# Cross attention with a recurrent scan: a shorter warm-up over states kept by column, an earlier check, and a projection that runs five groups ahead

## The chip, the cores and the metric

One core of a Trainium2 chip runs the kernel. Its engines work beside each other: TensorE (PE, matmuls; PEld is its weight load), VectorE (DVE), ScalarE (ACT), GpSimd (POOL), and SyncE (SP), which issues DMAs. The metric is the device time in microseconds; lower is better.

## The reference

x (4096 tokens of 512) attends with 8 heads to a context of 3202 tokens; a second layer norm follows, a projection to 64 numbers per token, and a recurrence over all tokens:

```python
x = residual + _mha(layernorm(x), layernorm(ctx), W_qkv, b_qkv, W_o, b_o)
residual = x
U = (layernorm(x) @ W_in.T + b_in) @ Bmat            # [T, 64]
def step(s, u_t):
    s = silu(s @ A.T) + u_t
    return (s, s)
_, states = scan(step, zeros, U)
x = residual + states @ Cmat
return x + (ctxb.mean(axis=1) @ W_prog.T + b_prog)
```

## The kernel before, in words

Attention comes first, 32 units of 512 queries and a pair of heads. Its outputs are scaled by the reciprocal of the sum of weights, split into a high and a low part (ost) and stored to o_scratch. The last unit's output is still on its way when the next stage begins: fold_den, invert and spread_rden turn its sum, scale_o (GpSimd) scales, high_o (ScalarE) and low_o (GpSimd) split, store_o (SP) stores. Groups 14 and 15 of the next stage can be loaded only after that store.

**Projection stage**, 16 groups (d) of 256 tokens, each in two halves. SP loads og(d), the attention output, into one of 3 slots, and x into xb. GpSimd adds the output bias to xb (add_bias). TensorE projects (24 matmuls, two PSUM banks; each half waits until VectorE has emptied the half before). VectorE adds xb into x1 and runs the norm's statistics and 13 tiny operations (an inverse root), which give the scale ya and the bias nmr. ScalarE applies them (norm2, into the one xn), TensorE transposes (turn2), ScalarE copies to nt (take_n2), and for every second group TensorE multiplies by w_u (finish) and ScalarE writes u twice (take_u): to u_low, the lower half of su, and to u_high. In TensorE's order project(d+3) stands before turn2(d). Some small work is hung on given groups: the sum over ctxb (VectorE, L1024), its matmuls, and c1, c2.

**Scan.** 4096 tokens are 256 chunks (NCH) of 16 (LCH). Step k handles token k of all chunks at once: a matmul of [u; v] (the 128 partitions of su) by A twice stacked, then a silu into v of the next column. Halves of 128 chunks alternate between two banks. The first sweep starts each chunk from zero; column 15 hands its result to the next chunk's column 0; the second sweep repeats all columns from there, and VectorE adds u to v for the states. A check compares the last column's v of both sweeps with 2^-38 of the squared norm of the states, by a matmul with ones, and writes a flag. All three engines read it; if it fails, the 4095 steps run one by one. Last, the states are split (s1, s2), multiplied with c1, c2, added to x1 and stored.

What orders all this is each engine's own queue, written out by hand, with semaphores.

## Time and profile before

| | |
|---|---|
| median of 3 runs | 2356.67 us (2354.91 to 2357.35) |
| profiled execution | 2354.21 us, its span 2351.9 us |
| attention, up to the projection | 2118.6 us |
| projection stage with its tail | 2118.6 to 2279.4 |
| scan | 2279.4 to 2316.0 |
| check and flag | 2316.0 to 2323.0 |
| final sums and stores | 2323.0 to 2351.9 |
| mean granted clock of TensorE | 0.98 |

The time of an execution is its span plus what lies around it. Busy time alone says little here: each stage has its own limit. The stages' borders are read from the timeline.

### The profile page before, as it was taken

The page shows a single profiled execution, that of the slowest core. Times are in us where ns is not written, and L with a number is a line of the kernel's source. Part 1 is how long each engine was busy: PE and PEld are TensorE (multiplying, and loading weights), DVE is VectorE, ACT ScalarE, POOL GpSimd, SP SyncE. Part 2 cuts the span into 40 slices and gives each one's busy share as a digit, 9 for nine tenths or more (in the row PEclk, how much of TensorE's full clock was granted, in tenths as well). Part 3 has the DMA queues.
Part 4 walks back from the last instruction along what each step waited for, and adds up shares of the span by engine and source line. Part 5 has one row for each costly group of instructions (what it writes and reads, how often), then busy time and mean ns, then how long its engine had stood idle before and what let it go on. Part 6 is the DMA issues. An engine that isn't in the chain of part 4 may idle for free.

```text
span 2351.9 us, 35969 instructions
## 1 busy us (share of the span) xinstructions
PE 2277.1 (97%) x14148; PEld 1321.2 (56%) x14148; DVE 1732.7 (74%) x2167; ACT 1121.4 (48%) x1429; POOL 1583.7 (67%) x1039
## 2 busy tenths in 40 slices
PE   8999989999999999999999999999999999998877
PEld 8998854555555545555555555555555555446653
DVE  5865546788888777888888887888887888646645
ACT  3654424454444444544454444544444445542354
POOL 1200026888888888888888889888888888884201
PEclk8999999999999999999999999999999999999987
DMA  6650225777677777776777777776777767877513
GB/s 241 217 177 10 81 74 120 155 155 156 155 154 160 172 164 171 174 159 153 164 158 178 165 174 170 155 155 154 156 157 159 155 154 162 188 174 220 171 45 143
DMA packets 158678, 365.01 MB, mean 155 GB/s; under 512 B 22511, under 2 KB 62063, under 8 KB 157870
## 3 DMA queue, kind: packets, MB, share of 16 engines
q0 software_dynamic: 59904, 218.13, 45.4%
q1 hardware_dynamic: 98606, 144.58, 19.0%
q8 instruction: 112, 1.84, 0.3%
q14 instruction: 56, 0.46, 0.1%
HBM read 95.41 MB, written 49.02 MB: 61 GB/s over the span
## 4 chain that ended last, share of the span: by engine, by line
PE 83%; POOL 4%; DMA 4%; issue 4%; DVE 3%; ACT 2%; SPq 0%; ACTq 0%; DVEq 0%; POOLq 0%
PE ps L1269 28%; PE ps L1142 10%; PE ps L1244 7%; PE ps L1246 7%; PE ps L1248 7%; PE ps L1106 4%; PE ps L1236 4%; DMA acca<-pt 3%; POOL accp L526 3%; PE ps L1124 3%; PE ps L1114 3%; PE ps L1333 2%; PE ps L1390 1%; PE ps L1087 1%; DVE mx_part L892 1%
## 5 line engine op out<-in xcount | busy, mean ns | idle before, releaser
L708 ACT ACTIVATE pt<-ps 128x1024 f32<-128x1024 f32 x800 | 779.1, 1021 | 909.3 <-PE ps L1248 886.1
L892 DVE TENSOR_REDUCE mx_part<-ps 128x2 f32<-128x1024 f32 x768 | 938.5, 1222 | 347.6 <-PE ps L1142 347.6
L526 POOL TENSOR_TENSOR accp<-accp,pt 128x1024 f32<-128x1024 f32 x416 | 1037.1, 2493 | 233.4 <-ACT pt L708 230.9
L1269 PE MATMUL ps<-pt,v 128*64 128x512 f32 x3328 | 805.9, 605 | 0.0
L965 DVE TENSOR_TENSOR ps<-ps,shb 128x1024 f32<-128x1024 f32 x403 | 493.2, 1224 | 51.8 <-PE ps L1248 51.8
L1269 PEld LDWEIGHTS ps<-pt,v 128*64 128x64 f32 x3328 | 202.2, 136 | 344.2 <-issue 336.4
L1142 PE MATMUL ps<-kk,qh 64*128 64x512 f32 x1536 | 350.0, 451 | 9.9 <-DVE mx_part L892 9.9
L1142 PEld LDWEIGHTS ps<-kk,qh 64*128 64x128 f32 x1536 | 143.5, 183 | 367.2 <-DVE mx_part L892 266.6
L1244 PE MATMUL ps<-qh,kk 64*128 64x512 f32 x1664 | 329.4, 391 | 4.9 <-ACT pt L708 4.9
L1248 PE MATMUL ps<-ql,kk 64*128 64x512 f32 x1664 | 329.7, 390 | 0.0
L1246 PE MATMUL ps<-qh,kk 64*128 64x512 f32 x1664 | 329.5, 391 | 0.0
L536 POOL DMA_DIRECT2D acca<-pt x192 | 182.5, 950 | 3.7 <-ACT pt L708 1.8
L1244 PEld LDWEIGHTS ps<-qh,kk 64*128 64x128 f32 x1664 | 157.9, 185 | 40.0 <-ACT pt L708 6.6
L1246 PEld LDWEIGHTS ps<-qh,kk 64*128 64x128 f32 x1664 | 158.2, 185 | 34.7
L1248 PEld LDWEIGHTS ps<-ql,kk 64*128 64x128 f32 x1664 | 158.2, 185 | 34.0
L1236 PE MATMUL ps<-sh,ones_row 64*128 64x512 f32 x858 | 173.9, 402 | 1.1 <-ACT pt L708 1.1
L515 POOL MEMSET sh<- 128x512 f32 x2 | 1.0, 530 | 187.2 <-PE ps L1124 187.2
L546 POOL DMA_DIRECT2D accb<-pt x128 | 126.3, 987 | 0.0
L1333 PE MATMUL ps<-wo_hl,og 128*128 128x512 f32 x384 | 98.8, 415 | 16.6 <-DVE x_first L1008 12.0
L1333 PEld LDWEIGHTS ps<-wo_hl,og 128*128 128x128 f32 x384 | 74.9, 199 | 38.5 <-issue 22.9
L571 POOL TENSOR_TENSOR xb<-xb,bo 128x512 f32<-128x512 f32 x32 | 40.7, 1324 | 81.0 <-DMA xb<-x 81.0
L1236 PEld LDWEIGHTS ps<-sh,ones_row 64*128 64x128 f32 x858 | 82.6, 187 | 15.2 <-ACT pt L708 12.5
(150 smaller groups left out, 1941.6 us busy)
## 6 DMA issues: line engine op xcount, KB each, us to landing
acca<-pt POOLq DMA_DIRECT2D x224, 512.0 KB, 4.9
accb<-pt POOLq DMA_DIRECT2D x160, 512.0 KB, 4.8
q_scratch<-kk SPq DMA_DIRECT2D x32, 512.0 KB, 4.4
acca<-accp POOLq DMA_DIRECT2D x32, 512.0 KB, 4.6
o_scratch<-ost SPq DMA_DIRECT2D x32, 512.0 KB, 3.1
og<-o_scratch SPq DMA_DIRECT2D x32, 512.0 KB, 5.8
shb<-m_scratch SPq DMA_DIRECT2D x31, 512.0 KB, 4.2
xs<-x SPq DMA_DIRECT2D x16, 512.0 KB, 6.5
```

Source lines behind the costliest of these rows:

```text
L526: nc.gpsimd.tensor_tensor(acc[:, :], acc[:, :], pt[n % PT_SLOTS][:, :], ALU.add).then_inc(added_p, 1)
L536: nc.gpsimd.dma_start(acc[:, :], pt[n % PT_SLOTS][:, :], accum_op=ALU.add).then_inc(added_a[u % 2], 16)
L708: nc.scalar.activation(pt[n % PT_SLOTS][:, :], src, ACT.Exp, scale=SCALE).then_inc(exped, 1)
L892: nc.vector.tensor_reduce(mx_part[:, m % QT, :, m // QT], src, AX_X, ALU.max).then_inc(max_taken, 1)
L965: nc.vector.tensor_tensor(ps[:, b:b + 2, :], ps[:, b:b + 2, :], shb[u % 2][:, :, :], ALU.add)\
L1142: ins = mm(ps[:, bank, :], q[r, (m % QT) * P:(m % QT + 1) * P], kk[r, p, 0, a:a + QB], start=True, stop=True)
L1236: ins = mm(ps[:, 2 * (t % 2) + h, :], ones_row[r, :], sh[u % 2][r, :], start=first, stop=not first)
L1244: mm(ps[:, b + h, :], kk[r, p, 0, key], qh[u % 3][r, :], start=first, stop=False)
L1246: mm(ps[:, b + h, :], kk[r, p, 1, key], qh[u % 3][r, :], start=False, stop=False)
L1248: ins = mm(ps[:, b + h, :], kk[r, p, 0, key], ql[u % 2][r, :], start=False, stop=last)
L1269: ins = mm(ps[HD * h:HD * (h + 1), 6, :], v[:, t, f:f + HD], pt[n % PT_SLOTS][:, h * QB:(h + 1) * QB], start=(t == 0), stop=(t == NT - 1))
L1333: ins = mm(ps[:, 2 + t, :], og[:, d % OG_SLOTS, a, k, rows], wo_hl[:, b, k], start=(i == 0), stop=(i == len(PASSES) - 1))
```

## The change

The first sweep begins at column 4 (SCAN_FROM) with v = 0, so 27 steps run instead of 31. su holds column k of all chunks side by side; take_u writes u_low in that order. The silu of column 4 (of zeros, so zeros) stands in ScalarE's queue after group 12. TensorE starts when the u_low copies are there. The check's bound comes from the first sweep's last column and its sum is begun early; the first two groups of states are split before the flag is read, and the fallback, which now has its own tile su_seq, splits them again. In the projection stage project runs 5 groups ahead, scales have 6 slots, VectorE adds group 1 before it norms group 0, and the small work hangs on other groups. OG_SLOTS stays at 3. The bodies of the fallback and the new semaphores' names are left out:

```diff
@@ -31,6 +31,8 @@
 
 X_SLOTS = 8
 OG_SLOTS = 3
+AHEAD = 5
+LN_SLOTS = 6
 
 QB = 512
 QT = QB // P
@@ -84,6 +86,9 @@
 
 LCH = 16
 NCH = T // LCH
+WARM = 12
+SCAN_FROM = LCH - WARM
+SCAN_TO = 2 * LCH - 1
 TOL2 = 2.0 ** -38
 
 MOD_LO = 96
@@ -219,9 +224,9 @@
         mv = small[:, 12:16].rearrange("p (t s) -> p t s", t=GT)
         ve = small[:, 16:18]
         yi = small[:, 18:20].bitcast(I32)
-        ya = small[:, 20:24].rearrange("p (s t) -> p s t", s=2)
+        ya = at("ya", [P, LN_SLOTS, GT], RR + 11776)
         yb = small[:, 24:26]
-        nmr = small[:, 26:30].rearrange("p (s t) -> p s t", s=2)
+        nmr = at("nmr", [P, LN_SLOTS, GT], RR + 11792)
         cu = [small[0:SD, 30:31], small[SD:2 * SD, 30:31]]
         pad = small[:, 31:32]
         bqkv = small[:, 32:44].rearrange("p (w c) -> p w c", w=3)
@@ -234,7 +239,8 @@
         bvb = at("bvb", [P, FC, P], 19456)
         x1_first = at("x1_first", [P, 10 * GT, H], 19968)
         x1_last = at("x1_last", [P, 6 * GT, H], 0)
-        su = at("su", [P, T + LCH], 30208)
+        su = at("su", [P, T], 30208)
+        su_seq = at("su_seq", [P, T], 10752)
         nt = at("nt", [P, 2, FC, GW], 34320)
         xn = at("xn", [P, GT, H], 36368)
         work = at("work", [P, 1024], 37392)
@@ -262,11 +268,13 @@
         u_low, v_all = su[0:SD, 0:T], su[SD:2 * SD, 0:T]
         end1 = work[SD:2 * SD, 0:NCH]
         diff = work[SD:2 * SD, NCH:2 * NCH]
-        ends2 = work[0:SD, 512:512 + NCH]
-        excess = work[0:SD, 768:768 + NCH]
-        uv_steps = su[:, 0:T].rearrange("p (c k) -> p k c", k=LCH)
-        v_steps = v_all.rearrange("p (c k) -> p k c", k=LCH)
-        v_next = su[SD:2 * SD, LCH:T + LCH].rearrange("p (c k) -> p k c", k=LCH)
+        ends = work[0:SD, 512:512 + NCH]
+        bound = work[0:SD, 768:768 + NCH]
+        excess = xn[0:SD, 0, 0:NCH]
+        u_tokens = u_low.rearrange("p (k c) -> p c k", c=NCH)
+        uv_steps = su[:, :].rearrange("p (k c) -> p k c", c=NCH)
+        v_steps = v_all.rearrange("p (k c) -> p k c", c=NCH)
+        v_seq = su_seq[SD:2 * SD, :]
         u_steps = u_high[SD:2 * SD, :].rearrange("p (c k) -> p k c", k=LCH)
         s_steps = s_all[0:SD, :].rearrange("p (c k) -> p k c", k=LCH)
 
...
@@ -462,7 +470,7 @@
                     load_og(d)
                 sp.wait_ge(x1_ready, GT * (d - 1))
                 load_x2(d)
-                if d == 6:
+                if d == 8:
                     fold_den(UNITS - 1)
                 if d == 7:
                     sp.dma_start(cb_sb[:, :, :], ctxb).then_inc(mod_loaded, 16)
@@ -471,7 +479,7 @@
                     sp.dma_start(c_aug[0:SD, :], cmat).then_inc(mod_loaded, 16)
                     for half in (0, 1):
                         sp.dma_start(at_sb[half * SD:(half + 1) * SD, :], a_t).then_inc(mod_loaded, 16)
-                if d == 9:
+                if d == 11:
                     spread_rden(UNITS - 1)
                 if d == 13:
                     store_o(UNITS - 1)
@@ -591,9 +599,9 @@
                 send_sum(u)
             for d in range(2, X_G):
                 add_bias(d)
-                if d == 10:
+                if d == 11:
                     scale_o(UNITS - 1)
-                if d == 12:
+                if d == 13:
                     low_o(UNITS - 1)
 
 
@@ -747,7 +755,7 @@
                 wait(act, n2_turned, 2 * d)
                 for t in range(GT):
                     ins = nc.scalar.activation(xn[:, t], x1(d)[:, t], ACT.Identity,
-                                               bias=nmr[:, d % 2, t:t + 1], scale=ya[:, d % 2, t:t + 1])
+                                               bias=nmr[:, d % LN_SLOTS, t:t + 1], scale=ya[:, d % LN_SLOTS, t:t + 1])
                 ins.then_inc(normed2, 1)
 
             def take_n2(d):
@@ -759,11 +767,16 @@
 
             def take_u(i):
                 act.wait_ge(u_done, i + 1)
-                for out_ in (u_low, u_high[SD:2 * SD]):
-                    for a in (0, 1):
-                        col0 = (2 * i + a) * GW
-                        ins = nc.scalar.activation(out_[:, col0:col0 + GW], ps[SD * a:SD * (a + 1), 6, 0:GW], ACT.Identity,
-                                                   bias=cu[a])
+                for a in (0, 1):
+                    d = 2 * i + a
+                    ins = nc.scalar.activation(u_tokens[:, d * GW // LCH:(d + 1) * GW // LCH, :],
+                                               ps[SD * a:SD * (a + 1), 6, 0:GW].rearrange("p (c k) -> p c k", k=LCH),
+                                               ACT.Identity, bias=cu[a])
+                ins.then_inc(u_low_ready, 1)
+                for a in (0, 1):
+                    d = 2 * i + a
+                    ins = nc.scalar.activation(u_high[SD:2 * SD, d * GW:(d + 1) * GW], ps[SD * a:SD * (a + 1), 6, 0:GW],
+                                               ACT.Identity, bias=cu[a])
                 ins.then_inc(u_ready, 1)
 
             for d in range(X_G):
@@ -773,8 +786,11 @@
                 take_n2(d)
                 if d == 0:
                     take_den(UNITS - 1)
-                if d == 6:
+                if d == 5:
                     high_o(UNITS - 1)
+                if d == 12:
+                    act.wait_ge(v_cleared, 1)
+                    nc.scalar.activation(v_steps[:, SCAN_FROM, :], v_steps[:, 0, :], ACT.Silu).then_inc(v_started, 1)
                 if d == 13:
                     act.wait_ge(mod_ready, 1)
                     act.wait_ge(c_cleared, 1)
@@ -784,28 +800,41 @@
             take_u(X_G // 2 - 1)
 
 
-            for k in range(2 * LCH - 1):
-                if k == 2 * LCH - 2:
-                    act.wait_ge(cmp_step, 1)
+            for k in range(SCAN_FROM, SCAN_TO):
+                if k == SCAN_TO - 1:
+                    act.wait_ge(cmp_step, 2)
                 for h, c in scan_halves():
-                    act.wait_ge(z_done, 2 * k + (h + 1))
-                    out_ = v_next[:, 0, c] if k == LCH - 1 else v_steps[:, (k + 1) % LCH, c]
-                    nc.scalar.activation(out_, ps[0:SD, h, 0:NCH // 2], ACT.Silu).then_inc(silu_done, 1)
+                    act.wait_ge(z_done, 2 * (k - SCAN_FROM) + (h + 1))
+                    z = ps[0:SD, h, 0:NCH // 2]
+                    if k == LCH - 1:
+                        n = min(c.stop + 1, NCH) - (c.start + 1)
+                        nc.scalar.activation(v_steps[:, 0, c.start + 1:c.start + 1 + n], z[:, 0:n], ACT.Silu).then_inc(silu_done, 1)
+                    else:
+                        nc.scalar.activation(v_steps[:, (k + 1) % LCH, c], z, ACT.Silu).then_inc(silu_done, 1)
+
+            def high_s(d):
+                src = s_all[0:SD, d * GW:(d + 1) * GW]
+                nc.scalar.activation(s1[0:SD, d % 2], src, ACT.Copy)
+                return nc.scalar.activation(s2[0:SD, d % 2], src, ACT.Copy)
+
+            act.wait_ge(st_ready, LCH)
+            for d in (0, 1):
+                high_s(d).then_inc(s_hi, 1)
             act.wait_ge(flag_ready, 1)
...
+            for d in range(2, X_G):
+                act.wait_ge(f_done, GT * (d - 1))
+                high_s(d).then_inc(s_hi, 1)
 
 
         @block.vector
@@ -1001,19 +1030,26 @@
                         nc.vector.tensor_tensor(bo[:, :], ps[:, 4, :], bo[:, :], ALU.add).then_inc(bo_ready, 1)
 
 
-            def project(d):
+            def add_x(d):
                 dve.wait_ge(xb_ready, d + 1)
                 for t in range(GT):
                     dve.wait_ge(y_done, GT * d + (t + 1))
                     nc.vector.tensor_tensor(x1(d)[:, t, :], ps[:, 2 + t, :], xb[:, d % 2, t], ALU.add)\
                         .then_inc(x1_ready, 1)
+
+            def norm2_scale(d):
                 dve.wait_ge(x1_ready, GT * (d + 1))
-                wait(dve, normed2, d - 1)
-                layernorm(d % 2, lambda t: x1(d)[:, t, :], ln2_ready)
-
+                wait(dve, normed2, d - LN_SLOTS + 1)
+                layernorm(d % LN_SLOTS, lambda t: x1(d)[:, t, :], ln2_ready)
+
+            add_x(0)
             for d in range(X_G):
-                project(d)
-                if d == 5:
+                if d == 0:
+                    add_x(1)
+                if d > 1:
+                    add_x(d)
+                norm2_scale(d)
+                if d == 7:
                     invert(UNITS - 1)
                 if d == 11:
                     dve.wait_ge(o_scaled, UNITS)
@@ -1027,6 +1063,8 @@
                     dve.wait_ge(mean_mm, 1)
                     nc.vector.tensor_scalar(mean[:, :], ps[0:SD, 7, 0:1], 1.0 / KEYS, None, ALU.mult)\
                         .then_inc(mean_ready, 1)
+                if d == 12:
+                    nc.vector.memset(v_steps[:, 0, :], 0.0).then_inc(v_cleared, 1)
                 if d == 14:
                     dve.wait_ge(mod_mm, 1)
                     nc.vector.tensor_tensor(c_aug[SD:SD + 1, :], ps[0:1, 7, :], bp[:, :], ALU.add).then_inc(mod_ready, 1)
@@ -1037,23 +1075,20 @@
 
 
             dve.wait_ge(u_ready, X_G // 2)
-            nc.vector.memset(v_steps[:, 0, :], 0.0).then_inc(st_ready, 1)
-
-            dve.wait_ge(silu_done, 2 * (LCH - 1))
+            dve.wait_ge(silu_done, 2 * (WARM - 1))
             nc.vector.tensor_copy(end1, v_steps[:, LCH - 1, :]).then_inc(cmp_step, 1)
+            nc.vector.tensor_tensor(ends, v_steps[:, LCH - 1, :], u_steps[:, LCH - 1, :], ALU.add).then_inc(cmp_step, 1)
+            dve.wait_ge(cmp_step, 2)
+            nc.vector.scalar_tensor_tensor(out=bound, in0=ends, scalar=-TOL2, in1=ends,
+                                           op0=ALU.mult, op1=ALU.mult).then_inc(cmp_step, 1)
             for k in range(LCH):
-                dve.wait_ge(silu_done, 2 * (LCH + k))
+                dve.wait_ge(silu_done, 2 * (WARM + k))
+                if k == LCH - 1:
+                    nc.vector.tensor_tensor(diff, v_steps[:, k, :], end1, ALU.subtract).then_inc(cmp_step, 1)
                 nc.vector.tensor_tensor(s_steps[:, k, :], v_steps[:, k, :], u_steps[:, k, :], ALU.add).then_inc(st_ready, 1)
 
-            nc.vector.tensor_tensor(diff, v_steps[:, LCH - 1, :], end1, ALU.subtract).then_inc(cmp_step, 1)
-            dve.wait_ge(st_ready, 1 + LCH)
-            ends = s_steps[:, LCH - 1, :]
-            nc.vector.tensor_tensor(ends2, ends, ends, ALU.mult).then_inc(cmp_step, 1)
-            dve.wait_ge(cmp_step, 3)
+            dve.wait_ge(cmp_step, 4)
             nc.vector.tensor_tensor(excess, diff, diff, ALU.mult).then_inc(cmp_step, 1)
-            dve.wait_ge(cmp_step, 4)
-            nc.vector.scalar_tensor_tensor(out=excess, in0=ends2, scalar=-TOL2, in1=excess,
-                                           op0=ALU.mult, op1=ALU.add).then_inc(cmp_step, 1)
             dve.wait_ge(sums_done, 1)
             nc.vector.tensor_reduce(flag_f[:, 0:1], ps[0:1, 2, 0:NCH], AX_X, ALU.max).then_inc(cmp_step, 1)
             dve.wait_ge(cmp_step, 6)
...
@@ -1357,24 +1397,24 @@
 
             pe.wait_ge(wo_lo, FC)
             pe.wait_ge(bo_ready, 1)
-            for d in range(OG_SLOTS):
+            for d in range(AHEAD):
                 project(d, 0)
                 project(d, 1)
             for d in range(X_G):
-                if d + OG_SLOTS < X_G:
-                    project(d + OG_SLOTS, 0)
+                if d + AHEAD < X_G:
+                    project(d + AHEAD, 0)
                 if d > 0 and d % 2 == 0:
                     finish(d // 2 - 1)
-                if d + OG_SLOTS < X_G:
-                    project(d + OG_SLOTS, 1)
+                if d + AHEAD < X_G:
+                    project(d + AHEAD, 1)
                 turn2(d)
                 if d == 0:
                     spread_sum(UNITS - 1)
-                if d == 8:
+                if d == 6:
                     pe.wait_ge(cb_summed, 1)
                     pe.wait_ge(den_taken, UNITS)
                     mm(ps[0:SD, 7, 0:1], cb_sum[:, :], ones[:, 0:1], start=True, stop=True).then_inc(mean_mm, 1)
-                if d == 10:
+                if d == 8:
                     pe.wait_ge(mean_ready, 1)
                     mm(ps[0:1, 7, :], mean[:, :], wp_sb[:, :], start=True, stop=True).then_inc(mod_mm, 1)
             finish(X_G // 2 - 1)
@@ -1382,24 +1422,29 @@
 
             pe.wait_ge(mod_loaded, 16 * 6)
 
-            pe.wait_ge(u_ready, X_G // 2)
-            pe.wait_ge(st_ready, 1)
-            for k in range(2 * LCH - 1):
+            pe.wait_ge(u_low_ready, X_G // 2)
+            pe.wait_ge(v_started, 1)
+            for k in range(SCAN_FROM, SCAN_TO):
                 for h, c in scan_halves():
-                    wait(pe, silu_done, 2 * (k - 1) + (h + 1))
+                    wait(pe, silu_done, 2 * (k - 1 - SCAN_FROM) + (h + 1))
                     mm(ps[0:SD, h, 0:NCH // 2], at_sb[:, :], uv_steps[:, k % LCH, c], start=True, stop=True)\
                         .then_inc(z_done, 1)
+            pe.wait_ge(cmp_step, 3)
+            mm(ps[0:1, 2, 0:NCH], ones[0:SD, 0:1], bound, start=True, stop=False)
             pe.wait_ge(cmp_step, 5)
-            mm(ps[0:1, 2, 0:NCH], ones[0:SD, 0:1], excess, start=True, stop=True).then_inc(sums_done, 1)
+            pe.wait_ge(cmp_step, 3)
+            mm(ps[0:1, 2, 0:NCH], ones[0:SD, 0:1], excess, start=False, stop=True).then_inc(sums_done, 1)
             pe.wait_ge(flag_ready, 1)
             good = pe.value_load(flag[0:1, 0:1], min_val=0, max_val=1)
             with pe.If(good == 0):
...
```

## Rows read from the trace of the kernel before

**Rows 1.** The page, the chain that ended last, its shares by line.
```profile
PE ps L1269 28%; PE ps L1142 10%; PE ps L1244 7%; PE ps L1246 7%; PE ps L1248 7%; PE ps L1106 4%; PE ps L1236 4%; DMA acca<-pt 3%; POOL accp L526 3%; PE ps L1124 3%; PE ps L1114 3%; PE ps L1333 2%; PE ps L1390 1%; PE ps L1087 1%; DVE mx_part L892 1%
```
**Rows 2.** Windows: stretch, length, busy us of each engine (instructions), clock, DMA share, GB/s.
```profile
2118.60:2260.00 141.40, 122.26 (x594) 93.76 (x592) 99.81 (x293) 45.32 (x78) 49.63 (x39) 0.95 0.58 179
2279.40:2316.00 36.60, 34.43 (x124) 17.07 (x124) 9.72 (x18) 24.67 (x64) 0.00 (x0) 0.58 0.00 1
```
**Rows 3.** TensorE's timeline: start, length, line, operation, count, idle time before.
```profile
2134.57 13.97 PE L1333 MATMUL ps<-wo_hl,og 128*128 128x512 f32 x48 [4.74 <-DVE x_first L1008]
...
2166.93 5.72 PE L1333 MATMUL ps<-wo_hl,og 128*128 128x512 f32 x24
2172.49 1.03 PE L1342 MATMUL ps<-ident,xn 128*128 128x128 f32 x8
...
2179.20 1.95 PE L1354 MATMUL ps<-nt,w_u 128*64 128x256 f32 x16
...
2194.37 4.58 PE L1333 MATMUL ps<-wo_hl,og 128*128 128x512 f32 x12 [3.06 <-DVE x_first L1008]
...
2224.62 0.28 PE L1376 MATMUL ps<-ones,cb_sum 128*64 128x1 f32 x2 [2.25 <-DVE cb_sum L1024]
```
**Rows 4.** VectorE's timeline, second norm of groups 5 and 6.
```profile
2169.58 1.29 DVE L855 BATCH_NORM_STATS2 small<-x_first 128x6 f32<-128x512 f32 x2 [2.54 <-ACT xn L749]
...
2172.05 1.20 DVE L824 TENSOR_SCALAR small<-small 128x2 int32<-128x2 int32 x1
...
2176.75 1.29 DVE L855 BATCH_NORM_STATS2 small<-x_first 128x6 f32<-128x512 f32 x2
...
2180.80 0.69 DVE L1008 TENSOR_TENSOR x_first<-ps,xb 128x512 f32<-128x512 f32 x1
...
2221.56 3.00 DVE L1024 TENSOR_REDUCE cb_sum<-cb_sb 128x64 f32<-128x1664 f32 x1
```
**Rows 5.** GpSimd's and SP's timeline, and DMA issues with median us to landing.
```profile
2170.70 2.52 POOL L571 TENSOR_TENSOR xb<-xb,bo 128x512 f32<-128x512 f32 x2 [5.55 <-DMA xb<-x]
...
2231.31 1.86 SPq L419 DMA_DIRECT2D og<-o_scratch  x2
...
o_scratch<-ost SPq DMA_DIRECT2D x32, 512.0 KB, 3.1
og<-o_scratch SPq DMA_DIRECT2D x32, 512.0 KB, 5.8
...
xb<-x SPq DMA_DIRECT2D x14, 512.0 KB, 3.9
```
**Rows 6.** Timeline of the tail, ScalarE and TensorE.
```profile
2260.74 1.52 ACT L749 ACTIVATE xn<-x_last,small 128x512 f32<-128x512 f32 x2
...
2270.54 1.52 ACT L749 ACTIVATE xn<-x_last,small 128x512 f32<-128x512 f32 x2
...
2274.00 3.46 PE L1354 MATMUL ps<-nt,w_u 128*64 128x256 f32 x16 [0.80 <-ACT nt L757]
```
**Rows 7.** Scan: table load; all silus (ns min/median/max, first and last start); last silus.
```profile
2279.44 1.28 ACT L793 ACT_TABLE_LOAD   x1
...
L793 ACT ACTIVATE su<-ps x62: 375/376/387, 2280.7 to 2315.6; 64x128 f32<-64x128 f32 x62
...
2315.22 0.76 ACT su L793 x2
```
**Rows 8.** Groups by form: an add over strided operands, a square over packed ones.
```profile
L1046 DVE TENSOR_TENSOR s_all<-su,u_high 64x256 f32<-64x256 f32 x16 | 9.6, 603 | 8.8 <-ACT su L793 8.8
...
L1053 DVE TENSOR_TENSOR work<-work 64x256 f32<-64x256 f32 x1 | 0.4, 419 | 0.0
```
**Rows 9.** Timeline from the flag to the final matmuls.
```profile
2320.25 0.14 DVE L1060 TENSOR_SCALAR flag<-flag_f 1x1 int32<-1x1 f32 x1
2321.35 0.42 ACT L807 ACTIVATE s<-s_all 64x256 fp32r<-64x256 f32 x1 [5.38 <-DVE flag L1060]
...
2323.01 0.77 PE L1411 MATMUL ps<-c,s 128*128 128x512 f32 x1 [3.24 <-POOL s L602]
```

28 lines of the change are left out of this document (17 added, 11 removed).

## The prediction

> **What bounds the kernel now.** I read the page first. Its chain by line [rows 1] gives nearly all shares to attention, which the change leaves alone. The edits touch what follows 2118.6 us, so I cut that by stage [rows 2]: the output projection with the second norm, up to 2260; its tail without projections, up to 2279.4; the scan, 36.6 us with TensorE's granted clock at 0.58; the check; the final sums. What is to be seen is that the stages have different limits.
>
> In the projection stage TensorE is busy 122 of 141 us. Its timeline [rows 3] shows the idle spots: 4.74 us before group 2, up to 3.06 us before every second group after that, 2.25 us for the sum over ctxb. A projected group costs 5.56 us (from the row at 2166.93 to the transposes at 2172.49), the transposes about 0.85, finish 1.9. VectorE's timeline [rows 4] shows why TensorE stops: the statistics of group 5 sat 2.54 us behind ScalarE's norm of group 3 (two slots of scales), one small operation then took 1.20 us where its kind takes 0.17 (it ran beside GpSimd's bias add [rows 5]), and the bank of the projection came free only after the last small operation. Undisturbed, a norm on VectorE takes 4.05 us (2176.75 to 2180.80) and the two adds 1.3.
>
> In the tail and the scan nothing is saturated; a chain of latencies passes from engine to engine [rows 6, 7]. The 31 scan steps take (34.9 - 0.43) / 30 = 1.15 us each, of which the two silus' 0.375 each are only a part.
>
> **The change, part by part.** *Scan length.* 27 steps instead of 31: -4 x 1.15 = -4.6 us, all on the path.
>
> *Scan layout.* The states of one step now lie side by side instead of 16 words apart. The trace has no silu that writes packed. VectorE gives the price: its add with every operand strided takes 0.603 us, its multiply of the same 64x256 with none strided 0.419 [rows 8], so 0.184 / 256 = 0.72 ns per element. ScalarE's strided 128 columns take 0.376 us while its packed copy of 256 takes 0.42 [rows 7, 9], so it seems to pay as well. At 0.72 ns, 128 elements give 0.09 us of each silu, and one silu lies in each step's loop: 27 x 0.07 to 0.09, I take 0.07 because the engine is another one: -1.9 us. Below stands 0 (silu is simply slow), above -2.4, and TensorE may gain too: it reads the same strided columns, one pass of 128 at 0.72 ns is 0.09 us, two passes 0.18, 27 steps -4.9 us. I take nothing for TensorE, because at a clock near 0.5 each column already takes it longer. Scan together: -6.5 us, between -4.6 and -11.9.
> The Trainium skill ("SBUF — State Buffer", Door 1: The DMA port swizzle) says that SBUF is read in lines of 16 bytes and that each access to a new line pays; a stride of 64 bytes pays on every element. VectorE's rows agree; for ScalarE "ScalarE: Activation LUTs" (What ACT_TABLE_LOAD costs) gives 186 ns + 0.833 ns per element, an estimate of 0.293 us for a packed silu, by which the layout would give 27 x 0.083 = 2.2 us instead of 1.9.
>
> *Start of the scan.* Before, the table load of 1.28 us stood between the last take_u and the first silu [rows 7]. Now the load and one silu over 256 columns (0.47, as the u copies of that size) stand in ScalarE's queue after group 12, and TensorE begins once the low copies are there, under the two high ones. The first silu follows take_u at once: -1.3 us here. The load is paid in the tail, below. The memset before it had run under the load and costs nothing, under VectorE's idle time now as well.
>
> *Check.* From the last silu's end (2315.98) to the matmul of the sums, VectorE ran an add, three products and a combination, 2.78 us. Now it runs the difference (0.42, both sides packed), the add (0.60) and one square (0.42), with gaps 1.5: -1.25 us. Bound and its matmul lie under the second sweep, where VectorE idles half of each step. Then the flag (2320.25 + 0.14). Before, ScalarE read it, began its copy at 2321.35, GpSimd subtracted, TensorE began at 2323.01 [rows 9]: 2.6 us. Now copies and subtractions of two groups run under the check (about 2.5 us, which is what the check still takes), and TensorE needs only its own read and branch. The trace has ScalarE's, 0.96; I take 1.1: -1.5 us, between -0.5 (a branch slower on TensorE) and -1.65. Check together: -2.75.
>
> *Projection stage.* It is three pieces. **Front**: five groups are projected before the first transposes. The second group's add now precedes the first norm, so group 2 follows without a gap and ends about 2135.8. But VectorE then owes two norms before it empties group 2: add of group 1 done 2130.7, norm 0 until about 2137.7 (4.05 and some 2.9 us beside the bias adds), norm 1 until 2141.8, then the add; TensorE restarts at 2142.6, a hole of 6.8 us where there were 4.74. Then VectorE sets the pace, 1.3 + 4.05 + about 1.1 for GpSimd = 6.5 us a group, and a low clock after the hole adds about 2. Group 5 is projected at 2163.3, before at about 2166.2, but then the transposes of 0 and 1, one sum and one finish (4.7 us) were already behind.
> **Middle**: up to the transposes of group 6 TensorE has 6 x 5.7 + 7 x 0.85 + 3 x 1.88 + 1.1 = 46.9 us, no norm waits for a slot, and VectorE's pair (2 x 6.5) stays under TensorE's 15: 2210. Before, a pair took 18 to 20. There the sum over ctxb is late: group 10's add 2201.4, norm 7.4 beside GpSimd, memsets 1.0, reduction 3.0: 2212.9, 3.0 us of idle time, and again 1.7 of low clock (12 matmuls in 4.58 instead of 2.9, row at 2194.37). Groups 12 and 13, a finish and two transposes end at 2229.5.
> Then a new wait: group 14 needs the last attention output from memory. Its low part now stands behind the bias add of group 13 instead of 12. Group 11's add 2214.1, transfer of x 3.9, bias add 2.5, low part 1.3, store 3.1, og issue and landing 6.3 [rows 5]: 2231.5, 2 us of idle time. Before, og was issued at 2231.31 and group 14 began 5 us after it had landed. The store is ahead of og on SP's queue, and x for group 14 behind both. Groups 14, 15, one finish, two transposes: 2246.6, before 2260.0.
> **Tail**: five groups (11 to 15) instead of three (13 to 15) run with nothing between them. A pair costs 9.8 us (2260.74 to 2270.54 [rows 6]); then comes the moved table load and silu, 1.75, with TensorE idle. So the tail takes 11.5 us more: 19.4 + 11.5 = 30.9, end of take_u 2277.5. The same bookkeeping, laid over the kernel before, ends some 5 us early, half of it at gaps with a low clock, which I have priced above; I put back 2 us: 2279.5 against 2279.4, so 0. A transfer of 1 us more goes through whole at group 14; the range of the stage is -5 to +5.
>
> Sum: 0 - 6.5 - 1.3 - 2.75 = -10.5 us. On the profiled execution (2354.21, span 2351.9 and 2.3 around it) that is 2343.7; the median of the runs lies 2.46 above it, so I forecast 2346.2.
>
> **The rivals.**
> - *The stage grows* (0.17). The hole of 6.8 us, the late og and the long tail are not made good: if the pairs of the middle keep VectorE's pace with GpSimd beside every norm (2 x 8 us instead of 15), five pairs end 5 us later, and og 2 more: +7, total -3.5, 2353. For it: VectorE's 1.20 rows. Against: the slots it waited for are now six.
> - *TensorE reads packed columns faster, or the clock rises early* (0.15): -4.9, and the middle hides the og wait, -2: total -17, 2339.
> - *The layout gives nothing* (0.10): -8.6, 2348.
> - *The silu table lacks Identity* (0.04): norm 13 reloads, the scan reloads: +2.6, total -8, 2348.7. The trace shows a Copy after the silus without a load, no Identity. The Trainium skill ("ScalarE: Activation LUTs", Table sets) says that identity and copy are in every set; by that this falls away.
> - *The check falls through* (0.03), the slower side. With 11 steps from zero before the first sweep's end instead of 15, the states must agree to 2^-19 = 1.9e-6 of a column's norm. If one chunk doesn't, 4095 single steps follow, none under 0.37 us of silu and 0.4 us of the way through TensorE: over 3 ms more. It decides at a ratio of 1.9e-6; the reference's recurrence, run on its own inputs in 32 bits, gives 2.4e-7 for the worst of 256 chunks (5e-8 from the first column). Eight times below, so unlikely, though table steps in the silu could lift it.
>
> **How the numbers follow.** The forecast has 0.51; its own range, from the stage's -5 to +5 and the scan's bounds, is 2340 to 2352. All cases: 2338 to 2353.5 leaves out 2 in 10. A measurement can tell 0.2% (4.7 us) from no change, so faster means below 2352.0. Faster: 0.46 of the forecast, 0.05 of the first rival, all of the second, 0.08 and 0.03 of the next two: 0.77. Slower: the check 0.03 and 0.04 of the first rival's far end: 0.07. Same: 0.16.
>
> **What the profile after would show.** The scan: 27 steps of 1.07 to 1.09 us, silus near 0.30; if they stay at 0.376 the layout gave nothing. A table load between groups 12 and 13, none before the scan. 1.5 us from last silu to sums, 1.1 from flag to TensorE. Stage: a hole of 6 to 7 us before group 3, few after, one near 2 us before group 14, transposes of group 10 near 2246 to 2249. The prediction is wrong if these transposes come after 2254, if group 14 waits 5 us or more, or if the scan's loop is not ScalarE's and TensorE's latencies.

## The result and the profile after

The changed kernel takes 2336.53 us (median of 4 runs, 2334.64 to 2339.71); the kernel before took 2355.93 beside it (4 runs, 2354.91 to 2357.35). The ratio is 0.9919 [0.9907, 0.9931], 19.4 us less. The forecast was 10.5 us less. The median lies 3.5 us under the forecast's own range (2340 to 2352) and 1.5 us under the range of all cases (2338 to 2353.5).

The profiled execution took 2339.71 us, span 2337.9, at a mean clock of 0.985. It is the slowest of its four, and the profiled one of before (2354.21) lies under all of its kernel's timed runs, so the two traces differ by 14.5 us only. Attention has the same code in both and scatters by several us from one execution to the next: the first projection matmul starts at 2118.66 before, at 2119.82 here, and in the other profiled executions anywhere from 2114.75 to 2123.70. So I count from that matmul.

| counted from the first projection matmul | before | after | difference | forecast |
|---|---|---|---|---|
| to the first silu of the scan | 162.1 | 162.9 | +0.8 | -1.3 |
| scan, to the end of the last silu | 35.2 | 22.0 | -13.2 | -6.5 |
| to the first final matmul | 7.03 | 3.97 | -3.1 | -2.75 |
| to the end of the span | 28.9 | 29.2 | +0.3 | 0 |
| sum | 233.2 | 218.1 | -15.1 | -10.5 |

The windows of [rows 2], cut at the borders of this execution (projection stage; tail; scan). The granted clock, as a mean of its two levels 0.50 and 1.00, is 0.96, 0.65, 0.92. In the scan before it was 0.58, and that is the first sign of what I missed:

```profile
2119.80:2248.20 128.40, 114.55 (x562) 88.61 (x560) 96.84 (x296) 41.93 (x68) 49.72 (x39) 0.96 0.62 197
2248.20:2282.70 34.50, 19.98 (x92) 12.50 (x92) 3.82 (x18) 23.32 (x37) 0.00 (x0) 0.65 0.00 0
2282.70:2304.69 21.99, 21.66 (x106) 10.66 (x106) 10.01 (x18) 14.44 (x54) 0.00 (x0) 0.92 0.00 1
```

TensorE's timeline, for [rows 3]. One hole of 7.21 us stands before group 3, then 2.31, 0.99 for the sum over ctxb and 1.84; before group 14 (the rows from 2232.04) there is none. Group 13's first half at 2220.91 takes 4.56 us where its kind takes 2.99; the mean clock there is 0.63:

```profile
2143.64 12.64 PE L1373 MATMUL ps<-wo_hl,og 128*128 128x512 f32 x48 [7.21 <-DVE x_first L1037]
2158.59 5.73 PE L1373 MATMUL ps<-wo_hl,og 128*128 128x512 f32 x24 [2.31 <-DVE x_first L1037]
2164.16 1.04 PE L1382 MATMUL ps<-ident,xn 128*128 128x128 f32 x8
...
2211.78 0.28 PE L1416 MATMUL ps<-ones,cb_sum 128*64 128x1 f32 x2 [0.99 <-DVE cb_sum L1060]
...
2220.91 4.56 PE L1373 MATMUL ps<-wo_hl,og 128*128 128x512 f32 x12 [1.84 <-DVE x_last L1037]
...
2232.04 5.75 PE L1373 MATMUL ps<-wo_hl,og 128*128 128x512 f32 x24
...
2246.07 1.03 PE L1382 MATMUL ps<-ident,xn 128*128 128x128 f32 x8
```

VectorE, for [rows 4]: in the hole two of its small operations take 1.10 and 1.18 us, as the 1.20 of before, beside GpSimd's add at 2138.82; the reduction takes 3.08.

```profile
2139.00 1.10 DVE L856 TENSOR_TENSOR small<-ya 128x2 f32<-128x2 f32 x1
2140.14 1.18 DVE L857 SCALAR_TENSOR_TENSOR small<-small 128x2 f32<-128x2 f32 x1
...
2208.64 3.08 DVE L1060 TENSOR_REDUCE cb_sum<-cb_sb 128x64 f32<-128x1664 f32 x1
```

SyncE and GpSimd, for [rows 5]: the low part at 2218.88, the store at 2220.17, and og at 2222.96.

```profile
2216.39 2.53 POOL L579 TENSOR_TENSOR xb<-xb,bo 128x512 f32<-128x512 f32 x2 [2.98 <-DMA xb<-x]
2218.88 1.26 POOL L574 TENSOR_TENSOR ost<-oraw,ost 128x512 fp32r<-128x512 f32 x1
```

```profile
2220.17 0.36 SPq L422 DMA_DIRECT2D o_scratch<-ost  x1
2222.96 0.91 SPq L427 DMA_DIRECT2D og<-o_scratch  x2
```

The tail, for [rows 6]. A pair of groups takes 11.47 us (xn at 2261.07 to xn at 2272.54), before 9.80. The copies that now write u_low in column order take 690 ns, before 469:

```profile
2252.10 3.68 PE L1394 MATMUL ps<-nt,w_u 128*64 128x256 f32 x16 [0.69 <-ACT nt L765]
...
2255.83 1.40 ACT L772 ACTIVATE su<-ps,small 64x256 f32<-64x256 f32 x2 [2.38 <-PE ps L1394]
...
2259.34 1.28 ACT L793 ACT_TABLE_LOAD   x1
...
2261.07 1.52 ACT L757 ACTIVATE xn<-x_last,nmr,ya 128x512 f32<-128x512 f32 x2
...
2272.54 1.52 ACT L757 ACTIVATE xn<-x_last,nmr,ya 128x512 f32<-128x512 f32 x2
...
2274.11 1.97 PE L1382 MATMUL ps<-ident,xn 128*128 128x128 f32 x8 [3.73 <-ACT xn L757]
```

```profile
L813 ACT ACTIVATE su<-ps x52: 256/269/270, 2282.7 to 2304.4; 64x128 f32<-64x128 f32 x52
...
L772 ACT ACTIVATE su<-ps,small x6: 683/690/703, 2255.8 to 2281.0; 64x256 f32<-64x256 f32 x6
```

That tile view also answers [rows 7]: 52 silus of 269 ns (two more have another line), before 376. One load of the table stands in the tail at 2259.34, none before the scan. ScalarE's timeline gives the steps, one silu of the same half to the next. The first took 0.80 us (2282.70 to 2283.50, the clock still high), the next three 1.04 to 1.05 at a clock of 0.50. Then come 14 silus in a row in 5.40 us, which is (5.40 - 0.65) / 6 = 0.79 us a step (0.65 is a pair at this pace), and 0.79 to the end:

```profile
2284.54 0.27 ACT L813 ACTIVATE su<-ps 64x128 f32<-64x128 f32 x1 [0.40 <-PE ps L1430]
...
2285.59 0.27 ACT L813 ACTIVATE su<-ps 64x128 f32<-64x128 f32 x1 [0.35 <-PE ps L1430]
...
2286.63 5.40 ACT L813 ACTIVATE su<-ps 64x128 f32<-64x128 f32 x14 [0.35 <-PE ps L1430]
```

For [rows 8], by form: the add still has two strided operands of three, the square packed ones.

```profile
L1088 DVE TENSOR_TENSOR s_all<-su,u_high 64x256 f32<-64x256 f32 x16 | 9.3, 591 | 2.4 <-ACT su L813 2.2
...
L1091 DVE TENSOR_TENSOR xn<-work 64x256 f32<-64x256 f32 x1 | 0.4, 417 | 0.0
```

For [rows 9], from the last silus to the final matmul. The bound's matmul at 2304.31 lies beside the last silus. Copies and subtractions of the first groups lie beside the check, and the final matmul follows the end of the flag (2307.36) by 1.30 us:

```profile
2304.10 0.59 ACT L813 ACTIVATE su<-ps 64x128 f32<-64x128 f32 x2 [0.20 <-PE ps L1430]
...
2304.31 0.59 PE L1433 MATMUL ps<-work,ones 64*1 64x256 f32 x2
2304.72 0.42 DVE L1087 TENSOR_TENSOR work<-su,work 64x256 f32<-64x256 f32 x1 [0.20 <-ACT su L813]
...
2305.68 0.42 DVE L1091 TENSOR_TENSOR xn<-work 64x256 f32<-64x256 f32 x1
...
2306.15 0.59 PE L1436 MATMUL ps<-xn,ones 64*1 64x256 f32 x2 [1.25 <-DVE xn L1091]
...
2306.59 1.40 POOL L610 TENSOR_TENSOR s<-s_all,s 64x256 fp32r<-64x256 f32 x2 [69.00 <-ACT s L818]
...
2307.22 0.14 DVE L1095 TENSOR_SCALAR flag<-flag_f 1x1 int32<-1x1 f32 x1
...
2308.66 0.77 PE L1456 MATMUL ps<-c,s 128*128 128x512 f32 x1 [1.93 <-POOL s L610]
```

### The profile page after: what moved, and what is told of

It is laid out like the page before. It is cut to its first block, busy times and chain, and to the rows that moved or that the text cites. A ratio compares the mean times of both kernels' runs of the same rounds, so it can differ in the third digit from the quotient of the medians.

```text
span 2337.9 us, 35932 instructions
## 1 busy us (share of the span) xinstructions
PE 2267.2 (97%) x14134; PEld 1311.6 (56%) x14134; DVE 1727.7 (74%) x2167; ACT 1117.8 (48%) x1422; POOL 1584.2 (68%) x1039
## 3 DMA queue, kind: packets, MB, share of 16 engines
q8 instruction: 112, 1.84, 0.3%
## 4 chain that ended last, share of the span: by engine, by line
PE 90%; DMA 3%; DVE 3%; issue 1%; ACT 1%; POOL 1%; SPq 0%; DVEq 0%; ACTq 0%; POOLq 0%
PE ps L1309 31%; PE ps L1182 11%; PE ps L1284 8%; PE ps L1286 8%; PE ps L1288 8%; PE ps L1146 4%; PE ps L1276 4%; PE ps L1164 3%; PE ps L1154 3%; PE ps L1373 3%; DMA acca<-pt 3%; PE ps L1127 1%; PE ps L1319 1%; DVE mx_part L921 1%; PE ps L1430 1%
```

## The experiments

All kernels start from the changed one, except `before_again`. Ratios are to the kernel before, run on the same chip. "First silu" is counted from the first projection matmul.

### The change again, and each of its three parts undone

`again` is the changed kernel, with no edit.

> The changed kernel once more, for its spread: four executions lay between 2334.6 and 2339.7 us, the profiled one at the top. Theory A: the spread is the moment at which TensorE's clock rises in the scan (a step costs 1.05 us before, 0.79 after), so a profile of a short execution shows more steps at 0.79 or fewer low stretches in the projection stage. Rival B: the spread lies in the transfers of the projection stage (the wait for og of group 14, the bias adds that hold up VectorE), and the scan is the same in every profile. Ratio expected 0.991 to 0.992.

`strided` keeps the chunks side by side instead of the columns, as before the change, and all the rest (27 steps, the early start, the check):

```diff
-        u_tokens = u_low.rearrange("p (k c) -> p c k", c=NCH)
-        uv_steps = su[:, :].rearrange("p (k c) -> p k c", c=NCH)
-        v_steps = v_all.rearrange("p (k c) -> p k c", c=NCH)
+        u_tokens = u_low.rearrange("p (c k) -> p c k", k=LCH)
+        uv_steps = su[:, :].rearrange("p (c k) -> p k c", k=LCH)
+        v_steps = v_all.rearrange("p (c k) -> p k c", k=LCH)
```

> The changed kernel with the states strided as before, 27 steps, all else as changed. Theory A (the packed columns raise the clock): the clock stays near 0.5 as it did in 28 of the 31 steps before, a step costs 1.15 us, the silu 0.376, the scan 31 us instead of 22, the kernel 9 us above the changed one, ratio 0.9955. Rival B (the clock rises for another reason, the shorter way into the scan): the step falls to the 1.10 us that the kernel before shows at the high clock, scan 29.8 us. Rival C (the layout itself gives nothing, only the clock): steps near 0.8 all the same, ratio 0.992.

`from_zero` runs all 31 steps, packed:

```diff
-WARM = 12
+WARM = 16
```

> The changed kernel with 31 steps from column 0, packed. If the step is 0.79 us with a high clock, the four steps cost 3.2 us (ratio up by 0.0013); if the clock is low for longer, up to 4 x 1.05 = 4.2 us. The forecast had 4.6 for them.

`three_ahead` puts the projection stage back: three groups ahead, two slots of scales, add and norm of a group together, the small work at its old groups; the scan and the check stay as changed.

```diff
-AHEAD = 5
-LN_SLOTS = 6
+AHEAD = 3
+LN_SLOTS = 2
...
-            add_x(0)
             for d in range(X_G):
-                if d == 0:
-                    add_x(1)
-                if d > 1:
-                    add_x(d)
+                add_x(d)
                 norm2_scale(d)
```

> The changed kernel with the projection stage as before (3 groups ahead, 2 slots of scales, the small work on its old groups), the table load still after group 12. Theory A, from the two profiles: the stage up to take_u costs the changed kernel 2.1 us more than before, so this one is 1 to 2 us faster than the changed kernel less 1.75 for the table load that stays: ratio 0.991. Rival B, from the times (median 19.4 us down, but the two profiles only 14.5 apart): other executions of the changed kernel gain 4 to 5 us in the stage, and this one is 3 to 5 us slower than the changed kernel, ratio 0.993 to 0.994.

| | median us | ratio | first silu | scan | silus end to final matmul |
|---|---|---|---|---|---|
| before, same chip | 2358.41 | 1 | | | |
| again | 2342.07 | 0.9929 [0.9915, 0.9942] | 161.0 | 22.0 | 4.0 |
| strided | 2349.63 | 0.9962 [0.9948, 0.9976] | 161.7 | 30.2 | 4.1 |
| from_zero | 2344.83 | 0.9945 [0.9931, 0.9958] | 158.3 | 25.1 | 4.0 |
| three_ahead | 2342.79 | 0.9936 [0.9922, 0.9949] | 163.2 | 21.8 | 4.4 |

The layout is worth 8.2 us of scan (30.2 to 22.0) and 7.6 of the medians, not 1.9. The length is worth 3.1 us in the packed scan (25.1 to 22.0, four steps of 0.79) and 5.0 in the strided one (35.2 before, 30.2 here). The stage of before, put back, differs from the new one by less than the intervals. So the error sits in the layout.

The profiled execution of `again` (2335.96 us, the shortest of its five, against 2339.71) has the same scan, 22.0 us, and the clock fell and rose at the same moments in it. So the spread is not in the scan, against theory A of `again`: the way to the first silu was 1.8 us shorter and attention 1.7. `three_ahead` has the ratio of its rival B, but not for B's reason: `again` gained nothing in the stage by which `three_ahead` could be slower.

The silus of `strided` and its TensorE:

```profile
L1430 PE MATMUL ps<-su,at_sb x108: 381/406/476, 2280.7 to 2311.0; 128*64 128x128 f32 x108
L813 ACT ACTIVATE su<-ps x52: 375/376/399, 2281.6 to 2311.5; 64x128 f32<-64x128 f32 x52
```

Over 26 steps, 0.107 us of silu makes 2.8, of 8.2. The rest isn't ScalarE's. The windows of `strided` show the clock: 0.50 from 2284 to 2300, then 1.00.

```profile
2284.00:2300.00 16.00, 16.00 (x57) 8.03 (x56) 4.04 (x8) 10.38 (x29) 0.00 (x0) 0.50 0.01 2
2301.00:2311.00 10.00, 9.71 (x38) 3.53 (x38) 5.70 (x10) 6.84 (x18) 0.00 (x0) 1.00 0.00 0
```

### Whose columns were slow, the writer's or the reader's

`reads_strided` keeps the silus packed and lets TensorE's scan matmuls read strided columns of x1_first's first groups, which nothing writes at that time:

```diff
+        idle_steps = x1_first[:, 0:8, :].rearrange("p a b -> p (a b)").rearrange("p (c k) -> p k c", k=LCH)
...
-                    mm(ps[:, ...], at_sb[:, :], uv_steps[:, k % LCH, c], ...)
+                    mm(ps[:, ...], at_sb[:, :], idle_steps[:, k % LCH, c], ...)
```

> Every scan matmul reads 128 columns 16 words apart from a tile that nothing writes (x1 of groups 0 to 3) instead of the states; the silus write packed. The states are therefore not those of the reference; all instructions and waits are the same. It takes TensorE's share of the layout by itself. Theory A (TensorE can't read strided columns faster at the high clock): silu 0.27 us, step 1.05 us at the low clock as in the changed kernel, about 0.99 at the high one instead of 0.79; the clock rises late, as in the run with all strided (after some 17 us). Rival B (all of the layout's gain is the silu's and the clock's): 0.79 at the high clock.

`writes_strided` is `strided` with TensorE reading packed columns of the same idle tile (`"p (k c) -> p k c", c=NCH`). In both the states are not those of the recurrence; waits, counts and sizes are.

> The mirror of it: the silus write 16 words apart, the scan matmuls read packed columns of the same idle tile; the states are not those of the reference. Silu 0.376 us. Theory A: step 1.15 us at the low clock, 0.79 + 0.107 = 0.90 at the high one. If the moment at which the clock rises depends on how TensorE reads, it rises within 5 us as in the changed kernel; if it depends on the length of the step alone, it rises late, as with all strided.

Each ran once: 2337.47 us with a scan of 26.6, and 2342.09 with 24.1. TensorE's matmuls (first lines) and the silus, by tile, `reads_strided` and then `writes_strided`:

```profile
L1431 PE MATMUL ps<-x_first,at_sb x108: 381/395/475, 2275.0 to 2301.7; 128*64 128x128 f32 x108
```

```profile
L1431 PE MATMUL ps<-x_first,at_sb x108: 272/273/325, 2281.4 to 2305.6; 128*64 128x128 f32 x108
```

```profile
L814 ACT ACTIVATE su<-ps x52: 375/376/399, 2282.3 to 2306.0; 64x128 f32<-64x128 f32 x52
```

A step of the scan, by who is strided and by the granted clock (steps read from ScalarE's timelines, one silu of a half to the next; the third and fourth column are the median silu and TensorE's median record):

| silus write | TensorE reads | silu | record | step at clock 0.50 | step at 1.00 |
|---|---|---|---|---|---|
| strided | strided | 0.376 | 0.394 | 1.154 | 1.09 to 1.10 |
| packed | strided | 0.268 | 0.395 | 1.045 | 0.985 |
| strided | packed | 0.376 | 0.273 | 1.154 (`idle_reads_packed`, below) | 0.90 |
| packed | packed | 0.269 | 0.273 | 1.045 | 0.79 |

The 0.394 is that of `busy_strided` (below), whose scan runs at the full clock throughout. At 1.00 the two effects add: packed silus give 0.105 to 0.11 a step, packed reads 0.19 to 0.20. At 0.50 packed reads give nothing: 1.045 with them and without, 1.154 with them and without. The window of the first five steps of `reads_strided`: the clock was high for the first and the last (0.99 us each) and low for the three between (1.05 each), so its mean is 0.67. In `writes_strided` the clock was at 1.00 on entering and stayed there, so it could not tell when the clock rises.

```profile
2275.90:2281.00 5.10, 4.91 (x21) 2.60 (x20) 0.00 (x0) 2.57 (x11) 0.00 (x0) 0.67 0.00 0
```

### The clock and the idle time ahead of the scan

`busy_gaps` fills TensorE's waits with 128x512 matmuls whose result nothing reads: 24 before group 3, 8, 22 and 14 before the transposes of groups 11, 13 and 15, 5 before the scan.

```diff
+            def keep_busy(n):
+                for _ in range(n):
+                    mm(ps[:, 0, :], wo_hl[:, 0, 0, 0:P], wo_hl[:, 0, 1], start=True, stop=True)
...
+                if (d, t) == (3, 0):
+                    keep_busy(24)
...
+                keep_busy({11: 8, 13: 22, 15: 14}.get(d, 0))
...
+            keep_busy(5)
             pe.wait_ge(u_low_ready, X_G // 2)
```

> The changed kernel with matmuls that nobody reads (128x512 into bank 0) in TensorE's queue where the profile shows it idle: 24 before group 3, 8, 22 and 14 before the transposes of groups 11, 13 and 15, 5 before the scan. Theory A (the low clock after each idle stretch is part of the tail's price): finishes of 1.9 us instead of 3.5, the scan at 0.79 from its first step, 4 to 6 us less than the changed kernel, ratio 0.990. Rival B: the added matmuls run at the low clock and hold up what they stand before, 3 us more, ratio 0.994.

`busy_strided` has the same extra matmuls, and the columns strided as in `strided`:

> The kernel with strided states (27 steps) and the matmuls in TensorE's idle spots, so that the scan begins at the high clock. Theory A (TensorE's granted clock follows how much of a step it works, and a strided step leaves it idle too long): the first steps cost 1.10 us, then the clock falls and they cost 1.15, scan 30.5 us. Rival B (what matters is only how the scan is entered): it stays high, every step 1.10, scan 29.8.

`before_again` is the kernel before, to see how its clock rises in another execution:

> The kernel before once more, for a second profile. The first matmul of the projection stage began at 2118.7 us before and, in six kernels whose attention is the same, between 2114.8 and 2123.5. Theory A: this spread belongs to attention and is here too, while the stretch from there to the first silu stays at 162.1 us within 1 us and the scan at 35.2. Rival B: the attention of the changed kernel alone varies.

`busy_gaps` takes 2333.51 us, 0.9887 [0.987, 0.9903]: with `busy_to_end` (below) the fastest kernel here, under the changed one's 0.9919 and 0.9929, and 7.1 us under `low_at_12` (below), which is the changed kernel but for the place of the low part and ran on the same chip. In its profile the first silu comes after 152.9 us (the changed kernel's two: 162.9 and 161.0), the scan takes 21.1. The clock is 1.00 from the tail to the end of the scan, and transposes take 1.09 us where the changed kernel had 1.97, finish 1.95 instead of 3.5 to 3.7. TensorE's timeline of the tail, the extra matmuls on L1370:

```profile
2254.99 1.09 PE L1389 MATMUL ps<-ident,xn 128*128 128x128 f32 x8 [0.84 <-ACT xn L757]
2256.88 1.95 PE L1401 MATMUL ps<-nt,w_u 128*64 128x256 f32 x16 [0.80 <-ACT nt L765]
...
2261.05 3.46 PE L1370 MATMUL ps<-wo_hl 128*128 128x512 f32 x14
2265.16 1.09 PE L1389 MATMUL ps<-ident,xn 128*128 128x128 f32 x8 [0.65 <-ACT xn L757]
```

`busy_strided` (2339.62 us, one execution) has a scan of 29.4 us and 1.09 to 1.11 a step. In the scan its clock never fell:

```profile
2274.30:2303.60 29.30, 28.36 (x108) 10.05 (x106) 10.61 (x18) 20.38 (x54) 0.00 (x0) 1.00 0.00 0
```

`before_again` (2352.66 us, one execution) has a scan of 34.3, and its first silu comes after 160.6 us where the first profile of before had 162.1, more than the 1 us that was expected. Its clock rose at about 2292, 12 us into the scan; in the first profile of before it rose some 30 us in. At these steps that is a difference of 0.9 us, all that an early clock gives the strided scan: (1.154 - 1.10) x 16 steps more. So neither half of the second rival would have done it alone. The early clock in the strided scan is worth a microsecond, packed reads without the clock nothing; in the packed scan both together are 0.255 a step (1.045 to 0.79).

### Does the layout bring the clock

Three kernels have 24 small copies in ScalarE's queue before the first silu, so that they would enter the scan alike. `idle_packed` is the changed kernel with them:

```diff
             take_u(X_G // 2 - 1)
+            for j in range(24):
+                t, col = (1, 32 * j) if j < 16 else (0, 32 * (j - 8))
+                nc.scalar.activation(xn[0:SD, t, col:col + 32], ps[0:SD, 6, 0:32], ACT.Copy)
```

> The changed kernel with 24 small copies (64x32, nothing reads them) in ScalarE's queue between the last take_u and the first silu, some 5 us in which TensorE idles, so that the scan surely begins at a low clock. If the packed layout itself brings the clock back, it rises 3 to 5 us after the first silu, as in the changed kernel (3.4 us of low clock), and the scan takes 22 to 23 us. If the early rise came from what TensorE did in the tail (a stretch at 1.00 just before), it comes later here, after 10 us or more, and the scan takes over 24 us (a low step is 1.045, a high one 0.79).

`idle_strided` is `strided` with them:

> The same 24 copies with all columns strided. If the layout decides, the clock is low for 12 us or more, as in the three strided executions seen (12, 18 and 30 us), and the step is 1.154 there. If the entry decides, the clock rises as many microseconds after the first silu as in idle_packed, to within 3 us, and the difference in the layouts' clock so far was chance.

`idle_reads_packed` is `writes_strided` with them:

> The same 24 copies; silus write strided columns, TensorE reads packed ones of an idle tile, so the states are not those of the recurrence. This fills the place that is empty in the table of steps: at a clock of 0.50. If packed reads give nothing at the low clock, as with packed silus, the step is 1.154 there. If what brings the clock is TensorE's reading and not the silus' length, it rises within 5 us of the first silu; if it is the length of a step, it stays low for 12 us or more, as when both are strided.

The copies took 2.1 us, less than I wrote. The clock was at 0.50 in all three at the first silu, but not for equally long: for 13.0 us in `idle_packed`, for 11.9 in `idle_reads_packed`, for 0.4 in `idle_strided`, where it had been at 1.00 for the 3.4 us before. The windows ahead of the first silu, `idle_packed` and then `idle_strided`:

```profile
2271.00:2282.40 11.40, 6.73 (x28) 3.99 (x28) 0.00 (x0) 6.07 (x32) 0.00 (x0) 0.50 0.00 1
```

```profile
2281.60:2285.00 3.40, 1.03 (x4) 0.50 (x4) 0.00 (x0) 3.33 (x27) 0.00 (x0) 1.00 0.01 2
```

| | silus | reads | one execution | low before the first silu | low after it | scan |
|---|---|---|---|---|---|---|
| idle_packed | packed | packed | 2339.26 us | 13.0 us | 4.1 us | 22.1 |
| idle_reads_packed | strided | packed | 2344.85 | 11.9 | 5.1 | 25.2 |
| idle_strided | strided | strided | 2350.91 | 0.4 | 16.7 | 30.2 |

The low stretches are read from short windows. The windows from 6 to 15 us after the first silu, in the order of the table:

```profile
2288.40:2297.40 9.00, 7.74 (x46) 4.39 (x46) 4.66 (x9) 6.00 (x24) 0.00 (x0) 1.00 0.01 2
```

```profile
2289.50:2298.50 9.00, 8.43 (x41) 3.81 (x41) 3.64 (x7) 7.57 (x21) 0.00 (x0) 1.00 0.01 2
```

```profile
2291.40:2300.40 9.00, 8.68 (x33) 4.61 (x32) 2.34 (x5) 5.80 (x17) 0.00 (x0) 0.50 0.01 2
```

These three don't separate the layout from the entry: counted from the moment at which the clock fell, it was low for 17.1 us in each. Other executions do, since they entered alike and differ in the layout. In `again` and `strided`, on one chip, the clock was at 1.00 for the last 3.4 us up to just after the first silu (0.7 and 1.8 us); then it was low for 3.4 us packed and for 17.1 strided. In `three_ahead` and `before_again` it had been low for 7.4 and 8.4 us at the first silu; it rose 2.8 us after it packed and 12.0 strided. And over all profiled scans that met the low clock, the nine in which the silus wrote or TensorE read packed columns ran at it for 2.8 to 5.1 us, the four with both strided for 12.0 to 30.5. So the layout has a part in when the clock rises. In `before` and `idle_strided`, both strided, the entries were alike as well, and the low stretches 30.5 and 16.7 us.

Nor is it the pace of the steps: until the clock rose, `idle_reads_packed` had the steps of 1.154 us of the strided scans. That TensorE's reading makes the difference rests on it alone, one execution whose entry is nearest to that of `before_again` (low for 11.9 and 8.4 us at the first silu, then for 5.1 and 12.0). And strided reads don't hold the clock down by themselves: `reads_strided`, with packed silus, had it back 4.3 us after the first silu.

`busy_to_end` is `busy_gaps` with 4 extra matmuls (into bank 3) before the matmul of the squares and 7 before the flag is read:

> The kernel with unread matmuls in the gaps, and 4 and 7 more around the check (before the matmul of the squares and before the flag is read). If the low clock costs the final matmuls time, these run at 1.00 from the start, and the part from the first final matmul to the end takes 27.3 us instead of 28.9: 1.6 to 1.8 us less than with the gaps alone, a ratio near 0.988. If VectorE's adds and the stores set the pace there, the ratio stays at 0.9887; if the extra matmuls delay those of the check, silu's end to final matmul grows from 4.2 us and the ratio rises to 0.989 or more.

It takes 2331.94 us, 0.9888 [0.9872, 0.9905], the same as `busy_gaps`. The final part did become shorter, 27.3 us against 28.9, and silu's end to final matmul stayed at 4.0; but in its profile the first silu came after 155.5 us instead of 152.9, with a gap of 1.84 us before group 13 and a low clock behind it that `busy_gaps` lacked. The gain is of the size of that scatter.

### Two changes of order in the projection stage

`low_at_12` puts the last unit's low part back behind the bias add of group 12:

```diff
-                if d == 13:
+                if d == 12:
                     low_o(UNITS - 1)
```

> The changed kernel with the low part of the last attention output after the bias add of group 12 as before, not 13. The forecast had 2 us of idle time before group 14 for this; the profiles of the changed kernel show none there (og landed before it was wanted) and 1.84 us before group 12 from VectorE instead. Theory A: no change against the changed kernel, ratio 0.992 to 0.993. Rival B: 2 us less.

It takes 2340.61 us, 0.9913 [0.9897, 0.993], the same as the changed kernel; first silu after 160.7. The wait for og that the low part was to cause did not exist to be removed.

`add_first` lets VectorE add group d+1 before it norms group d, all along:

```diff
-                if d == 0:
-                    add_x(1)
-                if d > 1:
-                    add_x(d)
+                if d + 1 == 12:
+                    dve.wait_ge(o_scaled, UNITS)
+                if d + 1 < X_G:
+                    add_x(d + 1)
                 norm2_scale(d)
```

> The changed kernel, but VectorE adds group d + 1 before it norms group d, for all groups. The hole of 7.2 us before group 3 stands because two norms (5.2 and 6.0 us) precede the add of group 2. Theory A: the hole goes, VectorE owes one norm less when TensorE wants the bank, and the stage ends 4 to 6 us earlier: ratio 0.990. Rival B: VectorE sets the pace of the front anyway, the hole moves to groups 4 and 5, nothing gained: ratio 0.9925.

`add_first_busy` is that with extra matmuls: those of `busy_gaps` without the 24, and 4 and 7 around the check.

> Both improvements: add of the next group before the norm, and matmuls that nobody reads in the idle spots of the tail, before the scan and around the check (8, 22, 14, 5, 4 and 7). If they add up: 6.5 us (run busy_gaps against low_at_12 on one chip) and 4 to 6 us, ratio 0.986. If the first fails, ratio 0.989.

`add_first` takes 2348.99 us, 0.9962 [0.9949, 0.9975], by the ratios slower than the changed kernel by 8 to 10. The hole before group 3 did go (1.21 and 1.05 us are left of 7.21 and 2.31), and the first transposes came at 2156.0. But TensorE then stood 11.85 us for the sum over ctxb and 6.12 for the mean:

```profile
2214.50 0.37 PE L1414 MATMUL ps<-ones,cb_sum 128*64 128x1 f32 x2 [11.85 <-DVE cb_sum L1058]
...
2237.65 1.86 PE L1417 MATMUL ps<-wp_sb,mean 64*1 64x512 f32 x2 [6.12 <-DVE mean L1062]
```

The reduction is hung behind norm 10, and TensorE's matmul of it stands ahead of the projection that the add of group 12 needs. Here VectorE had the add of group 11 and a norm more ahead of it, and finished the reduction at 2214.4. The small work would have to move to other groups as well; that wasn't tried. With the extra matmuls it takes 2341.80, 0.9934 [0.992, 0.9949], and has the same two waits (11.23, 6.13); the extra matmuls gave 7 us back, and the two waits kept it above `busy_gaps`.

## Why the prediction was wrong, point by point

**Scan layout: the step that failed.** "I take nothing for TensorE, because at a clock near 0.5 each column already takes it longer." At 0.5 that is what the runs show: 1.045 us a step with packed reads and with strided ones, against my 1.08 (1.15 less 0.07). The error was to hold the clock at its level of before, as if the layout had no part in it. The clock was low for 3 steps of the changed scan and high for 23; the pairs of executions that entered the scan alike show that the layout has its part in that. In numbers, strided at the low clock to packed, over 26 steps: silus 26 x 0.107 = 2.8 (I had 1.9, scaled down from VectorE's price; unscaled it gives 2.4). The clock, 23 x 0.06 = 1.4 (1.045 to 0.985). TensorE's packed reads, 23 x 0.195 = 4.5 (I had 0, with 4.9 as the upper bound). Together 8.7; `strided` to `again` measured 8.2, where 12 steps of `strided` already had the high clock (12 x 0.055 = 0.7). I had written this case down as a rival, but as two alternatives joined by an "or", and priced it at -17, with a chance of 0.15; the runs say "and". None of the three signs by which I would have called the prediction wrong came; the steps did (0.79 us where I had 1.07 to 1.09). The tail before had it in view: the same matmuls took 3.46 and 1.95 us [rows 6, 3], and the upper bound of 4.9 for TensorE was worked out and dropped on the clock's level alone.

The Trainium skill ("SBUF — State Buffer", Door 1: The DMA port swizzle) has every access to a new line pay. For ScalarE the runs agree: 0.84 ns an element (0.107 / 128), beside the 0.72 worked out from [rows 8] for VectorE. For TensorE they agree at the full clock only: at 0.50 strided reads added nothing to a step. "ScalarE: Activation LUTs" (What ACT_TABLE_LOAD costs) gave an estimate of 0.293 us for the packed silu; 0.269 was measured, and by its estimate the silus' part would have been 2.2 instead of the 2.8 found.

**Scan length.** Forecast -4.6, measured -5.0 strided (some of it clock). In the packed scan the same four steps are worth 3.1, so the two edits are not additive: each takes away part of what the other would save.

**Start.** Forecast -1.3, measured 1.30 (take_u's end to the first silu: 1.32 before, 0.02 after). One load stands in the tail, and Identity after the silu needed none, as the Trainium skill's rule on table sets has it ("ScalarE: Activation LUTs", Table sets); that rival is out.

**Check.** Forecast -2.75, measured -3.06. Flag to TensorE 1.30 us against my 1.1; the sums' matmul took 0.59 us at a clock of 1.00 where it had taken 1.01 at 0.50, which I hadn't counted. It didn't fall through.

**Projection stage.** Forecast 0 with -5 to +5. Counted to the end of take_u it is +2.1 (160.8 before, 162.9 after), and that is within the scatter: the second profile of before has 159.2, and four more executions of the new stage (`again`, `from_zero`, `reads_strided`, `low_at_12`) have 158.3 to 161.1. By its own steps: hole 6.8, measured 7.21; restart at 2142.6, measured 2143.64, which is 2142.5 when counted from the first matmul; reduction of 3.0 right, its wait 0.99 instead of 3.0; wait for og 2 us, none seen (the terms for og's landing add up to 2231.2, not to 2231.5 as written); transposes of group 10 at 2246.6, measured 2247.1, or 2245.9 counted so. The tail was forecast at 30.9 us and took 35.6. Two things are in that. The column-order copies of u_low cost 0.22 us more each, two in each of three pairs; I had costed the new order of u_low at nothing, although my own price for a stride was at hand. And the clock was 0.65 instead of the 0.83 that the tail of before (2260.0 to 2280.7) had, so that transposes took 1.97 instead of 1.09 and finish 3.68. The two microseconds that I put back for doubts, without naming them, covered less than half of these 4.7 us. The medians of `three_ahead` (0.9936) and `again` (0.9929) say that the whole rearrangement of the stage is worth nothing that can be measured. In the profiles TensorE gains in the middle what it loses in a hole and a longer tail. The first rival (the stage grows by 7) is out.

**The total.** -10.5 forecast. On the profiled pair the stage came out 2.1 worse, the scan 6.7 better, the check 0.3 better, the end 0.3 worse: -15.1 by the table. The rest of the -19.4 isn't the change's: attention began the stage 1.2 us later in the profiled run of after, 0.5 lies around the spans, the profiled run of before was 1.7 under its kernel's median (I had allowed for it), that of after 3.2 above. -15.1 + 1.2 - 0.5 - 1.7 - 3.2 = -19.3. Measured again on another chip the ratio was 0.9929, which is 16.7 us. So about 3 us of the 19.4 are not sure to be the change's, and the miss of the forecast is 6 to 9 us, of which the layout is 6.

**Open.** Why the clock rises early when either side is packed isn't explained. TensorE's busy time doesn't tell the cases apart in the low stretch (16.00 of 16.00 us in `strided`), and `busy_strided` shows that a strided scan doesn't bring a high clock down. Nor is it shown why the clock of before rose after 12 us in one execution and after 30 in the other.

## What to carry to other kernels

Price a step of a latency chain at both granted clocks before costing an edit of it at nothing: an edit of a layout in the chain can move the clock, and costs hidden at the low one (here 0.195 us of strided reads) appear at the high one. A reordered write costs its own stride: look for the other operations on the tile whose layout changes, not only for those in the loop. And where TensorE waits in a chain of latencies, unread matmuls in the waits can be worth more than a rearrangement of the work: 73 of them gave 7 to 10 us here (0.9887 against 0.9913 on the same chip, and 0.9919 and 0.9929 on others), the reordering none.

## What the runs showed of the hardware

- A strided read of fp32 columns (64 bytes apart) cost TensorE nothing at a clock of 0.50 and 0.195 us a step at 1.00, where the record of a 128-column matmul went from 0.395 to 0.273 us. So its cost isn't added to the columns' time at either clock; it shows only once the columns are read fast.
- Scans with strided silus and strided reads stayed at a clock of 0.50 for 12.0 to 30.5 us before it rose (four executions), scans with either side packed for 2.8 to 5.1 us (nine). At the same pace of steps (1.154 us) the one with packed reads took 5.1.
- ScalarE pays a stride for writing: silu of 64x128 0.376 to 0.269 us, a copy 64x256 to column order (1024 bytes apart) 0.690 against 0.469, and the silu of 64x256 from and to strided columns 0.626 against 0.412.
- Identical code in attention ended between 2114.75 and 2123.70 us in eighteen profiled executions, which is wider than most of the effects here: only stretches counted from a common instruction could be compared between single executions.
